# Post-norm attention layer on 8 cores: two weight conversions as single DMAs, and the ternary weight transposed by 64 DMA transposes ahead of the projections

## The reference, cut to what matters

```python
x = L0_attn_x                                     # (4, 4096, 1024) float32
# attention: 16 heads of 64, causal, rotary positions on Q and K
Q, K, V = split(einsum('bsi,oi->bso', x, W_qkv), 3)
attn = softmax(mask(rope(Q) @ rope(K).T / 8)) @ V
x = layernorm(x + einsum('bsi,oi->bso', attn, W_o))
# feed-forward: activations rounded to 8 bits, ternary weight minus one
x_dq = clip(round(x / scale), -127, 127) * scale
w = ternary_weight.astype(float32) - 1.0          # (1024, 1024) int32: 0, 1, 2
x = layernorm(x + einsum('bsi,oi->bso', x_dq, w) + bias)
```

## Time and profile before

| | us |
|---|---|
| runs of the kernel before | 1681.73 and 1736.41, median 1709.07 |
| the profiled execution | 1686.47 |
| its span (slowest core, core 7) | 1684.9 |
| spans of the other cores | 1664.5 to 1678.0 |

### The profile page before, as it was taken

One profiled execution on the slowest core, in us unless ns is written; L12 is line 12 of the kernel. 1 busy time (PEld: TensorE's weight loads), 2 busy tenths in 40 slices (PEclk: granted clock), 3 DMA queues, 4 the chain that ended last, 5 costly groups with the idle time before them and its releaser, 6 DMA issues.

```text
span 1684.9 us, 18237 instructions; the slowest of 8 cores (1664.5 to 1684.9 us)
## 1 busy us (share of the span) xinstructions
PE 1133.7 (67%) x5064; PEld 381.8 (23%) x5064; DVE 563.9 (33%) x1147; ACT 1003.5 (60%) x1259; POOL 43.3 (3%) x73
## 2 busy tenths in 40 slices
PE   1000899998976266777777878788888775656563
PEld 0000444444432011111111111112222212222221
DVE  1000233333344155333332222322112224666664
ACT  0000455554554267788888888888898874445443
POOL 1010000000000000000000000000000000000000
PEclk9999999999999577799999999999999987878876
DMA  5689466656632622322223132332222001111211
GB/s 101 110 134 166 105 146 137 148 141 139 119 69 62 120 68 79 104 91 82 96 91 119 60 113 84 112 123 79 78 79 79 1 11 40 61 65 51 75 50 50
DMA packets 113234, 153.30 MB, mean 91 GB/s; under 512 B 39152, under 2 KB 93424, under 8 KB 108784
## 3 DMA queue, kind: packets, MB, share of 16 engines
q1 hardware_dynamic: 66688, 117.46, 21.3%
q0 software_dynamic: 12912, 26.29, 10.8%
q10 hardware_dynamic: 33536, 8.39, 3.3%
HBM read 132.26 MB, written 46.14 MB: 106 GB/s over the span
## 4 chain that ended last, share of the span: by engine, by line
PE 44%; ACT 17%; DMA 13%; DVE 12%; issue 10%; ACTq 3%; DVEq 0%; POOL 0%; SPq 0%; POOLq 0%
ACT exp_b L508 13%; PE pAV L530 12%; PE pRaw L322 7%; PE pSC L493 7%; PE pC L380 7%; DVE exp_b L519 6%; DMA q_scr<-krot 5%; PE pR L636 5%; DMA wqkv_bf<-wqkv 4%; PE pR L723 4%; DMA maskb<-masks 2%; ACT recb L539 2%; DMA wo_bf<-wo_in 2%; ACTq L253 1%; DVE uf L706 1%
## 5 line engine op out<-in xcount | busy, mean ns | idle before, releaser
L508 ACT ACTIVATE exp_b<-pSC 128x1024 bf16<-128x1024 f32 x640 | 607.1, 1052 | 146.5 <-PE pSC L498 137.3
L530 PE MATMUL pAV<-exp_b,v_run 128*128 128x512 bf16 x1280 | 417.7, 412 | 93.2 <-DVE exp_b L519 92.2
L493 PE MATMUL pSC<-q_run,k_run 64*128 64x512 bf16 x640 | 254.1, 405 | 122.7 <-ACT exp_b L508 101.6
L519 DVE TENSOR_TENSOR exp_b<-exp_b,maskb 128x512 bf16<-128x512 bf16 x512 | 211.8, 425 | 370.2 <-ACT exp_b L508 306.0
L498 PE MATMUL pSC<-q_run,k_run 64*128 64x512 bf16 x640 | 259.2, 414 | 0.0
L493 PEld LDWEIGHTS pSC<-q_run,k_run 64*128 64x128 bf16 x640 | 57.6, 94 | 421.3 <-issue 421.3
L530 PEld LDWEIGHTS pAV<-exp_b,v_run 128*128 128x128 bf16 x1280 | 77.3, 98 | 277.3 <-issue 277.3
L328 ACT CAST kraw<-pRaw 128x512 bf16<-128x512 f32 x96 | 56.4, 587 | 122.9 <-PE pRaw L322 70.2
L322 PE MATMUL pRaw<-x_T,w_kvT 128*128 128x512 bf16 x512 | 124.6, 391 | 1.4 <-ACT x_T L310 1.4
L305 PE MATMUL pD<-identb,x_tm 128*128 128x128 bf16 x192 | 15.4, 226 | 152.5 <-DMA x_tm<-x_kv 99.5
L380 PE MATMUL pC<-w_kvT,x_T 128*128 128x512 bf16 x512 | 115.7, 379 | 0.0
(11 more groups left out here) (95 smaller groups left out, 912.5 us busy)
## 6 DMA issues: line engine op xcount, KB each, us to landing
v_scr<-v_stg SPq DMA_DIRECT2D x32, 512.0 KB, 3.6
v_run<-v_scr SPq DMA_DIRECT2D x8, 2048.0 KB, 7.8
v_run<-v_scr SPq DMA_DIRECT2D x8, 1536.0 KB, 7.0
x_tm<-x_kv POOLq DMA_DIRECT2D x16, 512.0 KB, 7.5
k_scr<-krot SPq DMA_DIRECT2D x64, 128.0 KB, 3.2
v_run<-v_scr SPq DMA_DIRECT2D x8, 1024.0 KB, 5.1
k_run<-k_scr SPq DMA_DIRECT2D x8, 1024.0 KB, 5.1
xo<-x_own SPq DMA_DIRECT2D x16, 512.0 KB, 4.2
```

Source lines behind the costliest of these rows:

```text
L493: s.add("T", (lambda sb_, bi, t: lambda te: te.matmul(pSC[sb_][:, 0:512], k_run[bi][0:64, t * 128:(t + 1) * 128], q_run[bi][0:64, :], star ...
L508: s.add("SC", (lambda eb, sb_: lambda sc: sc.activation(exp_b[eb][:, :], pSC[sb_][:, :], ACTF.Exp))(eb, sb_), reads=[f"pSC{sb_}"], writes= ...
L519: s.add("V", (lambda eb, moff, half: lambda v: v.tensor_tensor(exp_b[eb][:, half * 512:(half + 1) * 512], exp_b[eb][:, half * 512:(half + ...
L530: s.add("T", (lambda eb, bi, t, hh, n, pit: lambda te: te.matmul(pAV[pit][:, hh * 512:(hh + 1) * 512], v_run[bi][:, t * 256 + hh * 128: t ...
```

## The change

Three things change in the first phase.

1. `wqkv` is converted by one DMA in place of 12, and `wo_in` by one in place of 4.
2. `emit_wload` and `emit_wjob` are gone. All 8 blocks of the ternary weight are now prepared in one loop that stands in the list behind the 24 weight transposes and ahead of the jobs.
3. In that loop the 8 transposes per block are no longer done by TensorE. They are DMA transposes from `w_st` to `w_fT`, SBUF to SBUF, issued from ScalarE's queue, each 128 x 128 bf16; VectorE's copy from PSUM is gone with them. The cast and the subtraction stay.

```diff
-            for rb in range(12):
-                s.add("G", (lambda rb: lambda g: g.dma_start(
-                    out=wqkv_bf[rb * 256:(rb + 1) * 256, :],
-                    in_=wqkv[rb * 256:(rb + 1) * 256, :]))(rb), writes=["wqkv_bf"])
-            for rb in range(4):
...
+            s.add("G", lambda g: g.dma_start(out=wqkv_bf, in_=wqkv), writes=["wqkv_bf"])
+            s.add("G", lambda g: g.dma_start(out=wo_bf, in_=wo_in), writes=["wo_bf"])
             for c in range(8):
...
-            def emit_wload(ot):
+            for ot in range(8):
+                stg = w_st[ot % 2]
+                skey = f"w_st{ot % 2}"
                 wsb = ot % 2
                 s.add("SY", (lambda ot, wsb: lambda sy: sy.dma_start(
...
                 s.add("SC", (lambda wsb: lambda sc: sc.copy(w_stf[:], w_sti[wsb][:]))(wsb),
                       reads=[f"w_sti{wsb}"], writes=["w_stf"])
                 s.add("V", (lambda stg: lambda v: v.tensor_scalar(
                     stg[:], w_stf[:], -1.0, None, op0=ALU.add))(stg),
                     reads=["w_stf"], writes=[skey])
...
-                    s.add("T", (lambda pdst, stg, c: lambda t: t.transpose(
-                        pdst[:, c * 128:(c + 1) * 128],
-                        stg[:, c * 128:(c + 1) * 128], identb[:]))(pdst, stg, c),
-                        reads=[skey, "identb"], writes=[pkey])
...
-                s.add("V", (lambda dstv, srcv: lambda v: v.tensor_copy(dstv, srcv))(dstv, srcv),
-                      reads=[pkey], writes=["w_fT"])
+                    s.add("SC", (lambda stg, c, ot: lambda e: e.dma_start_transpose(
+                        w_fT[:, c * 1024 + ot * 128: c * 1024 + (ot + 1) * 128],
+                        stg[:, c * 128:(c + 1) * 128]))(stg, c, ot),
+                        reads=[skey], writes=["w_fT"], dma=True)
...
-            emit_wload(0)
-            emit_wload(1)
             emit_xtp(0, None)
...
-                if i < 8:
-                    emit_wjob(i)
-                    if i + 2 < 8:
-                        emit_wload(i + 2)
```

More of the change, by code:

```diff
@@ L234, in build_nc @@
                   reads=["pRaw2"], writes=["rs_bc"])
-            for rb in range(12):
-                s.add("G", (lambda rb: lambda g: g.dma_start(
-                    out=wqkv_bf[rb * 256:(rb + 1) * 256, :],
-                    in_=wqkv[rb * 256:(rb + 1) * 256, :]))(rb), writes=["wqkv_bf"])
-            for rb in range(4):
-                s.add("G", (lambda rb: lambda g: g.dma_start(
-                    out=wo_bf[rb * 256:(rb + 1) * 256, :],
-                    in_=wo_in[rb * 256:(rb + 1) * 256, :]))(rb), writes=["wo_bf"])
+            s.add("G", lambda g: g.dma_start(out=wqkv_bf, in_=wqkv), writes=["wqkv_bf"])
+            s.add("G", lambda g: g.dma_start(out=wo_bf, in_=wo_in), writes=["wo_bf"])
             for c in range(8):
@@ L262, in emit_wload @@
                     writes=[f"w_sti{wsb}"])
[L264 to L267, removed]
                 s.add("SC", (lambda wsb: lambda sc: sc.copy(w_stf[:], w_sti[wsb][:]))(wsb),
@@ L272, in emit_wjob @@
                     reads=["w_stf"], writes=[skey])
-                pdst = pD if ot % 2 == 0 else pE
-                pkey = "pD" if ot % 2 == 0 else "pE"
                 for c in range(8):
-                    s.add("T", (lambda pdst, stg, c: lambda t: t.transpose(
-                        pdst[:, c * 128:(c + 1) * 128],
-                        stg[:, c * 128:(c + 1) * 128], identb[:]))(pdst, stg, c),
-                        reads=[skey, "identb"], writes=[pkey])
-                dstv = w_fT[:].rearrange("p (ic c) -> p ic c", ic=8)[
-                    :, :, ot * 128:(ot + 1) * 128]
-                srcv = pdst[:, :].rearrange("p (ic c) -> p ic c", ic=8)
-                s.add("V", (lambda dstv, srcv: lambda v: v.tensor_copy(dstv, srcv))(dstv, srcv),
-                      reads=[pkey], writes=["w_fT"])
+                    s.add("SC", (lambda stg, c, ot: lambda e: e.dma_start_transpose(
+                        w_fT[:, c * 1024 + ot * 128: c * 1024 + (ot + 1) * 128],
+                        stg[:, c * 128:(c + 1) * 128]))(stg, c, ot),
+                        reads=[skey], writes=["w_fT"], dma=True)
             def emit_xload(i):
```

## The result

The changed kernel took 1798.7 us at the median of 11 runs (1790.3 to 1849.2), the kernel before 1682.0 us (10 runs, 1673.6 to 1736.4). The ratio is 1.068, with a 95% interval of 1.0654 to 1.0706: slower by some 115 us. The ratio leaves out executions in which the cores of one half of the chip ran at a lower granted clock than the rest. I had forecast 1773 us with a range of 1735 to 1840, and slower. The direction and the cause were right; the forecast rise, 87 us, was 28 us too small: the gain of the single conversions was taken 20 us too large, the chain of transposes 13 us too short.

What follows compares the result with a forecast made beforehand. The first x_T copy was taken to bound the start, TensorE the K jobs. Conversions -34, 64 chained transposes +149, wjobs -28 gave +87 us on 1686.5: 1773.5 us, range 1735 to 1840.

Steps and rivals of the forecast that it cites:

- What bounds the start: First x_T copy on ScalarE, after 165.0 us: whatever stands ahead of it moves the program's end one for one.
- Part 1, the conversions: Single DMAs for wqkv and wo: wo_bf ready at 68 us instead of 101.9, gain 34 us, between 6 and 40.
- I take 50, near the first end: Conversion of wqkv: wqkv_bf ready at 50 us, between 45 and 77, from 3.35 us a chunk.
- rival C: Conversions: DRAM limits eight cores copying without pause, gain 6 us and not 34, 1802 us; chance 15 in 100.
- Part 2, the chain of 64: DMA transposes on ScalarE's queue ahead of the x_T copy: 64 x 2.3 = 147 us, +149 with first cast and subtraction.
- so they hide, just: Ternary blocks: the seven later casts and subtractions fit behind the previous block's eighth transpose, 2.3 us, at no cost.
- Part 3, the wjobs: K jobs: without the wjob each projection follows the swap sooner, 3.5 us a job, 28 us for 8.
- Rivals A and B: A: round trip 1.16 us, total 1708 us, 10 in 100; B: 3.4 us, 1844 us, 10 in 100.

Runs made afterwards that it cites:

- e1: The kernel before with only the conversions changed, one DMA for wqkv and one for wo: ratio 0.9927, 1673.6 us.
- e7: The changed kernel launched on one core only, the other seven cores' work left out: 1729.3 us in one execution.
- e6: The kernel before with 8 chained DMA transposes replacing TensorE's at each K job's end: 1883.1 us, mean of the two shorter of four executions, against 1685.4.
- e4: The changed kernel with eight semaphores for the transposes into w_fT, so none waits for another inside a block: ratio 1.0390 to the kernel before, 1751.8 us.
- e3: The changed kernel with ternary blocks still ahead of the jobs, but transposed by TensorE with a VectorE copy per block: ratio 0.9872 to the kernel before.
- e10: As e3, with the ternary loop moved ahead of the 24 weight transposes, while the conversion runs: ratio 0.9825 to the kernel before.

## Why the prediction was right, and where its size was off

**What bounds the start: right.** The x_T copy moved by 148 us, and TensorE's wait with it.

**Part 1, the conversions: the term was mis-sized, -14 us and not -34.** The step that failed is "I take 50, near the first end, since the chunks' own rate inside a burst is a row of this trace". It gave 3.35 us a chunk and wqkv_bf at 50 us; back to back on eight cores it is 5.2 to 5.3 (e1, the changed kernel), and on one core 2.7 (e7). A burst rate from a kernel in which every core pauses 43% of the time is a rate at part load. The reasons given against rival C, that the cores ran their bursts side by side anyway, were an assumption that no row showed. Rival C had the mechanism, a rate that the cores share, and put it too strongly: 14 us of gain (10 in e1) stand between its 6 and the forecast's 34. A second thing was left out: wo_bf had landed at 86.9 us, but the first w_oT transpose was issued at 90.8, since the w_qT transpose ahead of it held the queue for 21 us.

**Part 2, the chain of 64: right in kind, 162 us and not 149.** The round trip, 2.3 us, was read off correctly: 2.29 measured. The step that failed is "so they hide, just". The last transpose of a block occupies ScalarE's queue for 1.10 us before the cast can start (196.44 to 197.54 in the chain above), where I had assumed a short issue; the next first transpose then starts 3.24 us after it and not 2.29. That is 0.95 us at each of seven seams between blocks, 6.6 us. Behind the last block it is the other way round: the x_T copy waits for the last issue and not for the landing, which saves 1.1. The other part is read from the trace only: in the first six blocks, which have an integer load in flight, the first transpose lands in 3.1 to 4.1 us; in the last two, which have none, in 2.23. With the same pattern in e6, where four rounds of a block are long while other DMAs are in flight, this is likely but not tested by itself. It comes to 7.3 us. The rounds themselves were 2.29 and not 2.3, 0.6 us in all. Together 6.6 - 1.1 + 7.3 - 0.6 = 12 us on core 5, where the x_T copy came 159.4 us after the first of the 64 was issued and 64 x 2.3 are 147. e4 shows that the waits for a landing are some two fifths of the cost and issuing most of the rest, and e3 that the method costs and not the place.

**Part 3, the wjobs: right, -31 us and not -28.** The 3.5 us came from one seam; what was left out is what the clock does after the pause. In the profile of before, core 7:

```profile
241.63 0.61 PE L276 MATMUL pE<-identb,w_st 128*128 128x128 bf16 x8 [2.84 <-DVE w_st L270]
242.08 5.30 PE L322 MATMUL pRaw<-x_T,w_kvT 128*128 128x512 bf16 x16
```

16 matmuls that take 3.62 us elsewhere took 5.30 here: the granted clock from 242.1 to 246 us was 0.59, so most of them ran at the lower of the two clock levels, 1.2 GHz. Core 7 has two such seams among its eight, 3.4 us together; on the other cores the slow seams come to 3.4 to 6.9 us, about the 3 us that the forecast lacks. After the change the seam between two jobs has no pause, and the clock stays at 1.00:

```profile
572.94 0.38 PE L317 MATMUL pSwp<-kraw,pswapb 128*128 128x512 bf16 x1
573.15 3.62 PE L306 MATMUL pRaw<-x_T,w_qT 128*128 128x512 bf16 x16
```

**Sum.** 87 + 20 (part 1) + 13 (part 2) - 3 (part 3) + 4 (Q projections) - 7 (attention) = +114 us, against some 115 measured. The last two terms were taken as nothing, and their causes stay open. Rivals A and B were both wrong: the round trip was neither 1.16 nor 3.4 us. In e6, though, beside the jobs' traffic, single transposes took up to 7.2 us to land. The Trainium skill's 1309 ns for a DMA transpose of 128 x 128 ("VectorE: DVE Perf Modes", section "The three transpose paths") would have given, as an estimate, 84 us for the 64 rounds; at 2.29 us each they took 147. It is close to the spacing in e4, 1.29 us, in which no transpose waits for another: as the price of one transpose in a stream it agrees, as the price of one that the next waits for it does not. The fixed cost of about 2.0 us in the Trainium skill's "DMA: Bandwidth & Descriptors", section "Anatomy of one DMA — SWDGE (gpsimd) path", came nearer, by 2.23 us measured for 32 KB; that section speaks of DMAs issued by GpSimd, and these were issued by ScalarE.

## What to carry to other kernels

Price a small DMA in a dependent chain by its time from issue to landing, and look at which engine's queue does the waiting: 64 round trips of 2.3 us were 147 us in which TensorE did nothing and the DMA engines were nearly idle. Letting them overlap took away 64 us, not all of it, since each still had to be issued. A rate read from bursts with pauses is no rate for the stream without them when the other cores do the same; bound it by a run with all cores and one with a single core. And a step that is cheap at one place in a queue is not so at another: the same eight transposes cost 20 us ahead of all work, and left TensorE idle for 27 us in the middle of it, beside other DMAs.

## What the runs showed of the hardware that I had not expected

- A DMA transpose of 128 x 128 keeps ScalarE's queue for 1.10 us, where one of 1024 rows kept it for 1.16 at least. Issuing does not shrink with the rows as I had thought.
- Eight cores copying without a pause take twice as long as one: 63.9 us against 32.2 for the same DMA.
- SyncE's load of 512 KB of integers lands in 4.5 us at the median in the kernel before and took up to 72 us beside a full software queue (e10).
- A DMA transpose of 128 x 128 in a chain lands in 2.23 to 2.29 us with little else in flight, and in 2.5 to 7.2 us beside a job's loads and writes (e6).
- In the kernel before, a pause of 2.8 us on TensorE was enough in some jobs for the next matmuls to run partly at the lower clock, 5.30 us in place of 3.62, and in others not.
